# The top-k layers of a mixed convolution and attention kernel, written anew as a line of 48 jobs on four engines

## The reference

```python
input_acts = _gelu(jnp.einsum('bsd,nd->bsn', x, input_patterns))
top_in_acts, top_in_idx = jax.lax.top_k(input_acts, K_INPUT)
input_repr = jnp.zeros((B, S, n_in), dtype=x.dtype).at[bi, si, top_in_idx].set(top_in_acts)
process_acts = _gelu(jnp.einsum('bsn,pn->bsp', input_repr, process_input_weights))
top_p_acts, top_p_idx = jax.lax.top_k(process_acts, K_PROCESS)
sel_values = process_values[top_p_idx]
p_weights = jax.nn.softmax(top_p_acts, axis=-1)
agg_value = jnp.einsum('bsk,bskd->bsd', p_weights, sel_values)
output_acts = _gelu(jnp.einsum('bsd,od->bso', agg_value, output_input_weights))
top_o_acts, top_o_idx = jax.lax.top_k(output_acts, K_OUTPUT)
sel_patterns = output_patterns[top_o_idx]
out = jnp.einsum('bsk,bskm->bsm', top_o_acts, sel_patterns)
```

## Time and profile before

| | us |
|---|---|
| median of three runs | 5954.21 |
| their range | 5950.46 to 6311.34 |
| the profiled execution | 5961.62 |
| its span, first to last instruction | 5959.8 |
| pattern stage, first weight load to last write of `H` | 2580.5 to 3986.1, 1405.6 |

### The profile page before, as it was taken

The page is one execution under the profiler, slowest core; times in us unless marked ns, Lnnn a source line. Parts: engine busy times, 40 slices in busy tenths (PEclk is TensorE's granted clock), DMA queues, the critical chain, the costliest instruction groups (busy, mean ns, idle before and its releaser), DMA issues. The chain is left out here.

```text
span 5959.8 us, 144342 instructions
## 1 busy us (share of the span) xinstructions
PE 4680.3 (79%) x57740; PEld 2937.0 (49%) x57741; DVE 3653.8 (61%) x10008; ACT 1932.3 (32%) x3675; POOL 485.6 (8%) x940
## 2 busy tenths in 40 slices
PE   3778888989798889845555655558999999997796
PEld 1257777734377777513333333324544454554564
DVE  3445444530254554459999999965868687884343
ACT  1133322311233332111121112114757576671221
POOL 0000000000000000000000000001111111110312
PEclk7878888979888898877777777778999999997897
DMA  1000000000000000000000000000000000003323
GB/s 38 2 7 3 3 3 3 3 16 0 6 3 3 3 3 3 4 34 1 0 0 0 0 0 0 0 1 9 0 1 0 1 0 1 1 0 122 118 79 100
DMA packets 47569, 85.79 MB, mean 14 GB/s; under 512 B 7120, under 2 KB 38128, under 8 KB 46064
## 3 DMA queue, kind: packets, MB, share of 16 engines
q1 hardware_dynamic: 40944, 61.84, 3.1%
q0 software_dynamic: 6144, 16.79, 0.9%
HBM read 45.05 MB, written 33.55 MB: 13 GB/s over the span
## 5 line engine op out<-in xcount | busy, mean ns | idle before, releaser
L1761 PE MATMUL psum<-hm_ex,hm_mix 128*128 128x512 f32 x1024 | 510.6, 621 | 42.2 <-ACT hm_Aq L1841 38.2
L1334 DVE TENSOR_SCALAR_CACHE_REDUCE pt_over<-pt_acts,pt_tb 128x1024 f32<-128x1024 f32 (+1 forms) x416 | 446.3, 1111 | 0.0
L1184 PE MATMUL psum<-K,pt_kept 128*128 128x128 f32 x512 | 96.2, 350 | 372.6 <-DVE pt_kept L1390 372.6
L1827 ACT ACTIVATE hm_ex<-psum,hm_nm 128x1024 f32<-128x1024 f32 x256 | 285.5, 1115 | 296.2 <-DVE hm_nm L1885 296.0
L1761 PEld LDWEIGHTS psum<-hm_ex,hm_mix 128*128 128x128 f32 x1024 | 175.6, 191 | 350.9 <-issue 343.2
L1900 DVE COPY hm_A<-psum 128x1024 f32<-128x1024 f32 x256 | 312.9, 1222 | 51.8 <-PE psum L1770 48.0
L1895 DVE TENSOR_SCALAR_CACHE_REDUCE hm_plus<-hm_Aq,hm_cbcol,hm_sums 128x1024 f32<-128x1024 f32 x256 | 340.4, 1330 | 0.0
L957 DVE TENSOR_TENSOR fw_M<-fw_M,psum 128x256 f32<-128x256 f32 x256 | 107.9, 421 | 345.2 <-PE psum L728 340.1
L1885 DVE TENSOR_REDUCE hm_nm<-psum 128x1 f32<-128x1024 f32 x256 | 311.0, 1215 | 12.1 <-PE psum L1749 12.1
L1770 PEld LDWEIGHTS psum<-K,hm_Aq 128*128 128x128 f32 x2048 | 236.6, 140 | 150.1 <-issue 145.3
L1195 PE MATMUL psum<-pt_w_proc,pt_keptT 128*128 128x512 f32 x512 | 265.5, 678 | 37.2 <-ACT pt_keptT L1263 37.2
(11 more groups left out here) (380 smaller groups left out, 9332.8 us busy)
## 6 DMA issues: line engine op xcount, KB each, us to landing
ex_rows_in<-ex_zero SPq DMA_DIRECT2D x2, 5120.0 KB, 24.5
ex_xs<-ex_rows_in SPq DMA_DIRECT2D x80, 128.0 KB, 2.1
ex_rows_out<-ex_ys SPq DMA_DIRECT2D x80, 128.0 KB, 1.7
ex_w<-in_ex_w SPq DMA_DIRECT2D x2, 4096.0 KB, 21.6
X<-in_x SPq DMA_DIRECT2D x2, 2048.0 KB, 12.6
out_y<-X SPq DMA_DIRECT2D x2, 2048.0 KB, 9.0
ff_w<-in_ff_w SPq DMA_DIRECT2D x2, 1024.0 KB, 5.9
pt_w_proc<-in_pt_proc SPq DMA_DIRECT2D x1, 2048.0 KB, 9.6
```

The source lines that it names most:

```text
L1334: both(lambda u: dve.tensor_scalar(over[:, u, 0:n], a(u), trial(u), 0.5 - keep, ALU.is_ge, ALU.add, accum_out=off(u)))
L1761: mm = pe.matmul(bank[4 + c], mix[:, u, :], ex[:, u, 512 * c:512 * c + 512], start=True, stop=True)
L1827: act.activation(ex[:, u, :], flat2(psum[:, 2 * u:2 * u + 2, :]), ACT.Exp, bias=nm[:, u:u + 1], accum_out=rsum[:, u:u + 1]).then_inc(s_ex, 1)
```

## The change

`pattern_stage` is written anew. A **job** is one layer of one pair of tiles; there are 48, numbered `j`, in sets of twelve: four pairs (four **lanes**) in the input layer, then the same four in the process layer, then in the output layer. The loop is gone: all engines walk through **slots** `s` from -1 to 50, unrolled. In slot `s`

- TensorE transposes what job `s - 3` kept and computes the scores of job `s + 1`; ScalarE applies their gelu;
- ScalarE **counts** for job `s` (counts 0 and 1) and, in the output layer, for job `s - 1` (count 2), by the sum of `Sign(value - trial)` (`count`), and GpSimd **narrows** after each of them (`narrow`, 11 operations for both tiles together, the division as a power of -1); `begin` sets up the first trial;
- VectorE does the last count and the closing of job `s - 2` (`close`), with the small operations for both tiles in one instruction, and keeps in place in `acts`.

So the counts are 3, 3 and 4 in all, of which VectorE does one. The kept values stand in `acts` itself, GpSimd's copies and `xt`, `kept`, `y` are gone, and ScalarE writes the result into `H` (`result`). The stage starts once `w_in` has arrived; the other weights are waited for in slot 3.

```diff
-    IN, PROC, OUT = (N_IN, 128, 4, 0), (N_PROC, 64, 4, 1), (N_OUT, 128, 5, 2)
+    LAYERS = ((N_IN, 128, 2), (N_PROC, 64, 2), (N_OUT, 128, 3))
+    LANES = 4
+    NJ = 3 * NT // 2
...
+        def counting(s):
+
+            return [(j, c) for j, c in ((s, 0), (s - 1, 2), (s, 1), (s - 1, 3))
+                    if 0 <= j < NJ and c < LAYERS[layer(j)][2]]
...
+                def narrow(j, c):
+
+
+                    l, n = layer(j), lane(j)
+                    bracket = tb[:, n, :, 2:6].rearrange("p u (b v) -> p u b v", b=2)
+                    pool.wait_ge(s_cnt, 2 * n_count[j, c])
+                    own.mark(pool.tensor_scalar(above[:, :, 0:1], tb[:, n, :, 1:2], float(middle(l)), None, ALU.is_gt))
...
+                    own.done(pool.tensor_tensor(bracket, bracket, db[:, :, :, :], ALU.add))
+                    own.mark(pool.tensor_tensor(df[:, :, :], tb[:, n, :, 2:4], tb[:, n, :, 4:6], ALU.subtract))
...
+                    own.mark(pool.tensor_tensor(slope[:, :], df[:, :, 1], minus[:, :], ALU.pow))
...
+                pool.wait_ge(s_num, 32)
+                for s in SLOTS:
+                    if 0 <= s < NJ:
+                        begin(s)
+                    for j, c in counting(s):
+                        narrow(j, c)
...
+                    for u in range(2):
+                        if n_count[j, c] > 1:
+                            act.wait_ge(s_cnt, 2 * n_count[j, c] - 3 + u)
+                        act.activation(signs[:, u, 0:n], acts[:, lane(j), u, 0:n], ACT.Sign,
+                                       bias=tb[:, lane(j), u, 0:1],
+                                       accum_out=tb[:, lane(j), u, 1:2]).then_inc(s_cnt, 1)
...
-                    for c in range(counts):
-                        both(lambda u: dve.tensor_scalar(over[:, u, 0:n], a(u), trial(u), 0.5 - keep, ALU.is_ge,
-                                                         ALU.add, accum_out=off(u)))
...
+                    dve.wait_ge(s_trial, n_count[j, counts - 1])
                     for u in range(2):
...
+                        own.mark(dve.tensor_scalar(over[:, u, 0:n], a(u), tb[:, lane(j), u, 0:1], 0.5 - keep, ALU.is_ge,
+                                                   ALU.add, accum_out=off[:, u:u + 1]))
...
+                            dve.scalar_tensor_tensor(a(u), a(u), kth[:, u, 0:1], a(u), ALU.is_ge,
+                                                     ALU.mult).then_inc(s_k, 1)
```

More of the change, by code:

```diff
@@ L1129, in _ @@
             def _(pool):
[L1130 to L1144, removed]
@@ L1158, in _, with begin @@
-                pool.wait_ge(s_h, 2)
-                chain.clear()
-                for n in range(4):
-                    if n >= 2:
-                        pool.wait_ge(s_a, n - 1)
-                    stage_tile(n, n % 2)
-                with pool.Fori(0, NR - 1) as i:
-                    round_(i)
-                round_(NR - 1, last=True)
-                pool.wait_ge(s_h, NT + 2)
+                own = Steps(pool, s_pch)
+                def begin(j):
+                    pool.wait_ge(s_g, n_act(j - 1, 1))
+                    n = lane(j)
+                    own.done(pool.tensor_tensor(
+                        first[:, :, :], start[:, layer(j), 0, :].unsqueeze(1).broadcast_to([P, 2, 6]),
+                        total[:, n, :].unsqueeze(2).broadcast_to([P, 2, 6]), ALU.mult))
+                    pool.tensor_tensor(tb[:, n, :, :], first[:, :, :],
+                                       start[:, layer(j), 1, :].unsqueeze(1).broadcast_to([P, 2, 6]),
+                                       ALU.add).then_inc(s_begun, 1)
@@ L1427, in _ @@
[L1427 to L1439 removed]
+                        own.mark(dve.scalar_tensor_tensor(side[:, u, 0:n], a(u), half[:, u:u + 1], over[:, u, 0:n],
+                                                          ALU.mult, ALU.add))
@@ new lines, in close @@
+                    own.done(dve.tensor_reduce(kth[:, :, 1], mine[:, :, :], AX.X, ALU.add))
+                    own.done(dve.tensor_tensor(kth[:, :, 0], kth[:, :, 1], half[:, :], ALU.mult))
+                    if layer(j) != PROC:
+                        sure()
+                        for u in range(2):
+                            dve.scalar_tensor_tensor(a(u), a(u), kth[:, u, 0:1], a(u), ALU.is_ge,
+                                                     ALU.mult).then_inc(s_k, 1)
+                        return
@@ L1442, in unsure_stage @@
+                own.mark(dve.memset(doubt[:, :, :], 0.0))
+                dve.wait_ge(s_num, 32)
+                for s in SLOTS:
+                    if 0 <= s - 2 < NJ:
+                        close(s - 2)
+                own.sync()
+                dve.wait_ge(s_yc, NT)
+                own.done(dve.tensor_reduce(unsure[:, :], doubt[:, :, :], AX.X, ALU.add))
 @stage
```

475 lines of the change are left out of this document (236 added, 239 removed).

## The result

| | us |
|---|---|
| before, median (4 runs of the same session) | 5970.77, from 5950.46 to 6311.34 |
| changed, median (4 runs) | 5358.73, from 5345.09 to 5380.74 |
| ratio, with its 95% interval | 0.899 (0.894 to 0.904) |
| profiled execution of the changed kernel | 5345.09, span 5343.3 |
| pattern stage, first weight load to last write of `H` | 802.2, before 1405.5 |

The changed kernel is 10% faster; the ratio leaves out the one execution of the kernel before that took 6311.34. Between the two profiled executions the span falls by 616.5 us, of which 603.3 are the stage's length. The first weight load stands 14.9 us earlier (2565.64 for 2580.55): 10 because it waits for `w_in` alone, as forecast, and 5 because the stages ahead ended sooner. What follows the stage took 1.7 more.

A forecast was written before the change was run, and what follows sets the result against it. VectorE, 90% busy, was taken to bound the pattern stage; the new slots sum as 56 + 4 x (66.4 + 69.9) + 3 x 71.9 + 49 = 866 us, ending 549 earlier: profiled 5413, median 5405, range 5315 to 5560.

The forecast's parts named there:

- the rival in which narrowing slips through: Pattern stage: no toll on GpSimd (3.3 us a narrowing), TensorE keeps its clock; stage 781, about 5320 us; chance 0.17.
- VectorE after: Pattern stage: VectorE keeps one count and one closing per job, 37.6 us a pair, 602 us against 1271.
- the earlier start: Stage start: first product waits only for `w_in`, 5.0 us after its issue, at 2571 instead of 2580.5.
- Input slots: Slots 3 to 6 of a set, input jobs turned: TensorE is the bound, 4 x 16.6 = 66.4 us.
- Process slots: Slots 7 to 10, process jobs turned: ScalarE, then a three-narrowing chain in slot 10, sets them; 69.9 us together.
- Output slots: Slots 11 to 14, output jobs turned: two by the narrowing chain, two by TensorE, plus 3.5; 71.9 us.
- The narrowing: GpSimd's chain between counts: 3.3 us of work, taken as 4.7 with hold-ups by VectorE's passes.
- the toll: VectorE's two-input passes, 37% of a slot, lock GpSimd out, raising a narrowing from 3.3 to 4.7 us.
- The clock: TensorE: full 2.4 GHz in eight slots of a set, 1.2 GHz in process slots, 3.5 us added per set.
- GpSimd as the bound: Pattern stage: a narrowing takes 7 us, so GpSimd's chain sets the slots; about 5558 us; chance 0.18.
- a clock of 0.75: TensorE's clock stays at 0.75 in the pattern stage: 933 us, about 5472 in all; chance 0.12.
- The second search: Pattern stage: a threshold over eight places away triggers `search_stage`, 3800 us more, about 9200; chance 0.03.

The follow-up runs named there:

- the idle products: Changed kernel with six idle 512-column products for TensorE after the transposes in the slots turning input jobs: 5411.52 us, ratio 0.909, stage 871.1.
- the idle powers: Changed kernel with two idle powers of -1 before the real one in each narrowing: 5469.38 us, ratio 0.917, stage 929.5.
- the two kernels: The changed kernel (5358.73 us), and the same with a product in place of the power in each narrowing, search branch left out (5354.29 us, ratio 0.892).

## Why the prediction was right

The forecast was right in direction and in the main mechanism: VectorE ceases to be the bound, TensorE and ScalarE's chain take turns. Its size was right for the whole, but the stage was put 64 us too long: the measured 802.2 is nearer to the 781 of the rival in which narrowing slips through than to the 866 of the forecast. The profiled execution lies 68 below its forecast (5345 for 5413); the median only 46 below, since the forecast took it 7 under the profiled one and it came out 14 above. Those 21 us are luck, and so is part of the fit of the narrowing, as said below. Term by term:

| term | forecast | measured |
|---|---|---|
| VectorE's work | 602 | 589 |
| first slots | 56 | 54.8 |
| four input slots | 66.4 | 63.9 |
| four process slots | 69.9 | 61.2 |
| four output slots | 71.9 | 64.2 |
| slots 39 to 46 | 136.3 | 132.3 |
| the end | 49 | 50.4 |
| start behind the issue of `w_in` | 5.0 | 4.95 |

- *VectorE after* came out within 13 us and *the earlier start* within a tenth. That VectorE would cease to be the bound was the main step, and the stage's length with the old number of counts (865) shows that it carries nine tenths of the gain.
- *Input slots.* TensorE is the bound, as said, and the idle products show it. 16.6 was the sum of the pieces of the earlier trace rows; they overlap, and from start to start a slot is 16.0.
- *Process slots.* More than half of the error, 8.7 us in each of four sets. Slot 7 was taken with the clock already low (16.3); TensorE comes straight from the input slots, both value products take 2.05 us together, and the slot is 12.9 (2872.85 to 2885.71). The next three are 16.4, 17.5 and 14.4, with value products of 3.8 for two tiles at the low clock, which were forecast at 4.1. The last was put at 17.4 by three narrowings of 4.7; they took 3.1, 5.0 and 3.1.
- *Output slots.* For two of four the chain of GpSimd was taken as the bound, 17.4. With narrowings of 3.6, 4.9 and 3.1 that chain is 14.9 and TensorE's 16 decides. The 3.5 us added once in a set for the clock's return were too much as well: by the copies, the first output slot takes 16.2 to 17.8 in the three sets and the next two 15.8. With 1.8 us more for a narrowing the chain does win (21.3 with the idle powers), so the mechanism was right and only its size off.
- *The narrowing,* the term of which both errors are made: 4.7 us forecast, 3.87 measured. Two faults stood against each other. The power costs 0.72, not 0.15, which alone adds 0.57. But a step is 0.28 from the one before, not 0.38 or 0.39, so the quiet narrowing is 3.09 all the same, less than the 3.3 forecast; and the toll is 0.78, not 1.4. The share of the passes was not what was wrong: those with two inputs (204 us) and L1408 and L1438 (79) are 35% of the stage, near the 37% assumed. But the narrowings lose 20% of their length to them. A part of the reason may be that VectorE's last count waits for the very narrowing (89 us before L1399); no run shows it.
- *The clock* in the process slots stayed low (0.77 granted), as the forecast said and the rival of 0.17 did not; but that rival's short narrowings (3.3) were the nearer ones. GpSimd as the bound and a clock of 0.75 are ruled out: TensorE, not GpSimd, sets the input and output slots, and the stage's clock is 0.90.
- *The second search* did not run. Its price was set at 3800 and is 4394 by one run that did it.

## What to carry to other kernels

Moving work off the engine that bounds a stage pays until the next chain, not until the next engine is full: GpSimd at 410 us of 802 was not far from being the bound, because eleven small operations in a row stand between two counts, and 1.8 us more for each such row cost 127. Count a small-operation chain by the start-to-start distance of its steps, and add what the neighbour's passes hold up. Where an engine waits for a product behind a pause, ask first whether something else of its own list can be done before it: that gave 22.3 us here, raising the clock 15.5, and it cost no work.

## What was not expected of the hardware

- A power on GpSimd over 128 x 2 float32 values takes 0.72 us with nothing beside it, a product 0.20 (L1174 in the two kernels). A reciprocal by power is thus as long as nearly four other small operations.
- The toll on GpSimd is not a slowdown but a wait for the end of a pass: operations beside VectorE's two-input passes of 1.28 us end with them (1.11 and 1.12 us for 0.19), even if they touch only four or eight values for each partition.
- VectorE's passes with one input and no sum (L1408, 0.81 us on the mean for 1024 values) hold GpSimd up as well (an operation of 0.19 took 0.64); those of one input with a sum (1.28 us) do not, as no operation of L1171 is longer than 0.65 us once they stand in place of the two-input ones.
